# An attention mask and a quantised feed-forward on one core: five instruction orders written anew, and rounding straight to float16

## The reference

```
sim  = (ctx Wq^T)(ctx Wk^T)^T * const             # 512 x 512 per sequence, heads summed
thr  = 153rd largest value of each row of sim
A    = sigmoid(sim) * (sim >= thr);  A = (A + A^T) / 2
x1   = x + (1 - g) * layernorm(x) + g * A           # g = sigmoid(gamma)
y    = layernorm(x1)
bitlinear(v, w): v = rmsnorm(v); v rounded to 255 levels by its row's largest |v|;
                 w rounded to {-1, 0, 1} by mean |w|;  product
out  = x1 + bitlinear(silu(bitlinear(y, w_gate)) * bitlinear(y, w_up), w_down)   # widths 512, 2048, 512
```

## Time and profile before

| | us |
|---|---|
| median of 3 runs (range) | 268.02 (267.92 to 268.54) |
| the profiled execution's own time | 268.02 |
| its span, first to last instruction | 266.2 |
| busy: PE, DVE, ACT, POOL | 216.5, 214.1, 194.6, 169.0 |
| mean granted TensorE clock | 0.91 of full |

### The profile page before, as it was taken

One profiled execution on the slowest core, in us unless ns is written; L12 is line 12 of the kernel. 1 busy time (PEld: TensorE's weight loads), 2 busy tenths in 40 slices (PEclk: granted clock), 3 DMA queues, 4 the chain that ended last, 5 costly groups with the idle time before them and its releaser, 6 DMA issues.

```text
span 266.2 us, 3714 instructions
## 1 busy us (share of the span) xinstructions
PE 216.5 (81%) x962; PEld 107.3 (40%) x974; DVE 214.1 (80%) x376; ACT 194.6 (73%) x333; POOL 169.0 (63%) x322
## 2 busy tenths in 40 slices
PE   7704620225998877999999999999999999999995
PEld 7301300222744432443445444434454444444434
DVE  0585987976869999898899999998898959367881
ACT  2499999899999999996949999736349443654030
POOL 2045787786988646678978878873886812505620
PEclk9965595555799999999999999999999999999999
DMA  4999999999655499420801382330714505743656
GB/s 128 394 374 360 360 230 397 242 317 214 182 113 86 79 178 159 80 59 1 140 1 28 52 139 61 79 68 19 194 37 101 102 0 100 173 133 71 119 101 216
DMA packets 79143, 39.19 MB, mean 147 GB/s; under 512 B 67984, under 2 KB 70544, under 8 KB 78608
## 3 DMA queue, kind: packets, MB, share of 16 engines
q1 hardware_dynamic: 79120, 38.94, 58.9%
HBM read 17.96 MB, written 4.19 MB: 83 GB/s over the span
## 4 chain that ended last, share of the span: by engine, by line
PE 30%; POOL 13%; POOLq 13%; DVE 11%; ACT 10%; issue 9%; DMA 6%; DVEq 4%; SPq 2%; ACTq 0%
PE U L405 9%; PE G L391 9%; PE DN L424 9%; DMA C<-in_ctx 5%; ACT junk_c L514 3%; POOLq L986 3%; ACT WuT L556 2%; POOL S L1047 2%; POOL qx L1016 2%; POOL X L982 2%; ACT S L563 2%; POOLq L948 2%; DVE S L764 2%; POOL sig L939 2%; POOLq L958 2%
## 5 line engine op out<-in xcount | busy, mean ns | idle before, releaser
L391 PE MATMUL G<-WgT,xqT 128*128 128x512 bf16 x256 | 60.5, 379 | 3.6 <-ACT sg L539 3.2
L539 ACT ACTIVATE sg<-G,gsc 128x1024 f32<-128x1024 f32 x32 | 35.5, 1110 | 37.2 <-PE G L391 34.8
L405 PE MATMUL U<-WuT,xqT 128*128 128x512 bf16 x256 | 60.5, 379 | 1.6 <-DVE S L764 1.6
L514 ACT ACTIVATE junk_c<-rows,srch 128x512 int8<-128x512 f32 (+1 forms) x76 | 53.8, 713 | 1.9 <-POOL srch L961 1.2
L764 DVE TENSOR_TENSOR S<-U,sg 128x1024 f32<-128x1024 f32 x31 | 37.9, 1222 | 13.0 <-PE U L405 7.7
L424 PE MATMUL DN<-WdT,S 128*128 128x512 bf16 x197 | 45.5, 379 | 0.9 <-DMA S<-S 0.3
L1047 POOL TENSOR_SCALAR S<-S,qh 128x2048 int16<-128x2048 f32 x15 | 30.0, 2002 | 25.1 <-DVE qh L829 24.9
L391 PEld LDWEIGHTS G<-WgT,xqT 128*128 128x128 bf16 x256 | 24.6, 98 | 35.1 <-issue 3.8
L547 ACT ACTIVATE junk_h<-S 128x2048 int8<-128x2048 f32 x16 | 30.5, 1905 | 10.2 <-DVE S L779 8.6
L405 PEld LDWEIGHTS U<-WuT,xqT 128*128 128x128 bf16 x256 | 24.8, 98 | 32.6 <-DVE S L764 4.3
L769 DVE TENSOR_REDUCE amh<-S 128x1 f32<-128x2048 f32 x15 | 34.1, 2271 | 0.1
(11 more groups left out here) (148 smaller groups left out, 370.4 us busy)
## 6 DMA issues: line engine op xcount, KB each, us to landing
S<-in_L_ffn_w_gate SPq DMA_DIRECT2D x4, 1024.0 KB, 9.2
S<-in_L_ffn_w_up SPq DMA_DIRECT2D x4, 1024.0 KB, 11.9
X<-in_x SPq DMA_DIRECT2D x4, 1024.0 KB, 10.8
S<-in_L_ffn_w_down SPq DMA_DIRECT2D x4, 1024.0 KB, 6.9
out<-X SPq DMA_DIRECT2D x15, 256.0 KB, 2.9
C<-in_ctx SPq DMA_DIRECT2D x2, 256.0 KB, 8.6
C<-in_ctx SPq DMA_DIRECT2D x1, 512.0 KB, 11.5
S<-S SPq DMA_TRANSPOSE x17, 4.3
```

The source lines that it names most:

```text
L391: last = nc.tensor.matmul(G[:, c * 512:(c + 1) * 512], xqT[:, t, k, :], WgT[:, 4 * n:4 * n + 4, k, :], start=(k == 0), stop=(k == KD - 1))
L405: last = nc.tensor.matmul(U[:, c * 512:(c + 1) * 512], xqT[:, t, k, :], WuT[:, 4 * n:4 * n + 4, k, :], start=(k == 0), stop=(k == KD - 1))
L514: A(junk_c[:, j, :].bitcast(U8) if r == ROUNDS else junk_c[:, j, :], ROWS[a % 2][:, j, :], ACT.Sign, bias=nthr[:, j:j + 1], accum_out=cs[: ...
L539: A(sg[:, u % 2, :], G[:, :], ACT.Silu, scale=gsc[:, b % 2, t:t + 1]).then_inc(silu_done, 1)
```

## The change

It has three parts. The number format: values that were rounded to an int16 integer n and then converted to bfloat16 n are now written once as float16 n * 2^-24, a multiple of that type's smallest step, so that the conversion on write does the rounding; the coefficients carry 2^24 in return. The casts `x_cast` and `h_cast` and the second instruction of `last_round` are gone, and those who waited for the int16 version or for the cast wait for the one rounding. Weights and transposed tiles are float16 in place of bfloat16. The orders: the lines of calls of all five engines are new. A wait: `x_stats` of sequence 1 to 3 now waits for the `ln_coef` of the sequence before (`ln_done`), as it can come earlier than before.

```diff
+UNIT = 2.0 ** -24
-        WgT = sb("WgT", [P, F // P, KD, P], BF16)
+        WgT = sb("WgT", [P, F // P, KD, P], F16)
...
-            w_load(0, w_gate, 0); w_load(0, w_gate, 1); w_load(0, w_gate, 2); w_load(0, w_gate, 3)
-            w_load(1, w_up, 0); c_load(0, 1, 2); c_load(1, 2, 4); x_load(0); w_load(1, w_up, 1)
+            w_load(0, w_gate, 1); c_load(0, 1, 2); w_load(0, w_gate, 0); w_load(0, w_gate, 2); w_load(0, w_gate, 3)
+            x_load(0); w_load(1, w_up, 2); x_load(2); w_load(1, w_up, 0); w_load(1, w_up, 1); w_load(1, w_up, 3)
...
                 if js[0] == 0:
                     dve.wait_ge(s_xin[a], 16)
+                    if a:
+                        dve.wait_ge(ln_done, a)
...
-            def x_cast(a, *js):
-                c = slice(js[0], js[-1] + 1)
-                dve.wait_ge(xi_ready, NT * a + js[-1] + 1)
-                V.tensor_copy(qx[:, c, :], qx[:, c, :].bitcast(I16)).then_inc(qx_ready, len(js))
...
-                V.tensor_scalar(hq[:, i % 2, f].bitcast(I16), h[:, i % 2, f], qh[:, i % 4:i % 4 + 1], 1.0,
-                                ALU.mult, ALU.mult)
-                dve.drain()
-                V.tensor_copy(hq[:, i % 2, f], hq[:, i % 2, f].bitcast(I16)).then_inc(hq_last, 1)
+                V.tensor_scalar(hq[:, i % 2, f], h[:, i % 2, f], qh[:, i % 4:i % 4 + 1], UNIT,
+                                ALU.mult, ALU.mult).then_inc(hq_last, 1)
...
-            def h_cast(i):
-                dve.wait_ge(hi_ready, i + 1)
-                V.tensor_copy(hq[:, i % 2, :], hq[:, i % 2, :].bitcast(I16)).then_inc(hq_ready, 1)
...
-                G_.tensor_scalar(gsc[:, a % 2, :], dx, wm[:, 0:1], 1.0, ALU.mult, ALU.mult)
+                G_.tensor_scalar(gsc[:, a % 2, :], dx, wm[:, 0:1], 1.0 / UNIT, ALU.mult, ALU.mult)
...
-                    G_.tensor_scalar(qx[:, j, :].bitcast(I16), ROWS[a % 2][:, j, :], qsx[:, j:j + 1], -1.0,
-                                     ALU.mult, ALU.mult).then_inc(xi_ready, 1)
+                    G_.tensor_scalar(qx[:, j, :], ROWS[a % 2][:, j, :], qsx[:, j:j + 1], -UNIT,
+                                     ALU.mult, ALU.mult).then_inc(qx_ready, 1)
...
-                G_.tensor_scalar(hq[:, i % 2, :].bitcast(I16), h[:, i % 2, :], qh[:, i % 4:i % 4 + 1], 1.0,
-                                 ALU.mult, ALU.mult).then_inc(hi_ready, 1)
+                G_.tensor_scalar(hq[:, i % 2, :], h[:, i % 2, :], qh[:, i % 4:i % 4 + 1], UNIT,
+                                 ALU.mult, ALU.mult).then_inc(hq_ready, 1)
```

More of the change, by code:

```diff
@@ L14 @@
 F32 = mybir.dt.float32
-BF16 = mybir.dt.bfloat16
+F16 = mybir.dt.float16
 I32 = mybir.dt.int32
@@ L457, in _ @@
             pe.wait_ge(s_msb, 1)
[L459 to L463, removed]
@@ L474, in _ @@
-            gate(31); down(11, 0); down(11, 1); up(30); down(12, 0); down(12, 1); up(31); down(13, 0); down(13, 1)
-            down(14, 0); down(14, 1); down_last(0); down_last(1)
+            pre(0); pre_g(0); sims(0, 0); sims(0, 1); sims(0, 2); sims(0, 3); pre(1); pre_g(1); sims(1, 0)
+            w_total(0); sims(1, 1); sims(1, 2); sims(1, 3); w_total(1); miss_total(0); a_transposes(0, 0)
+            a_transposes(0, 1); a_transposes(0, 2); a_transposes(0, 3); pre(2); warm(8, 0); warm(8, 1); gate(0)
@@ new lines, in _ @@
+            pre_g(2); up(0); sims(2, 0); miss_total(1); gate(1); up(1); w_total(2); sims(2, 1); gate(2); up(2)
+            gate(3); up(3); sims(2, 2); gate(4); a_transposes(1, 0); sims(2, 3); gate(5); a_transposes(1, 1); up(4)
+            gate(6); a_transposes(1, 2); a_transposes(1, 3); up(5); gate(7); up(6); down(0, 0); down(0, 1); pre(3)
+            up(7); down(1, 0); down(1, 1); pre_g(3); gate(8); up(8); gate(9); up(9); down(2, 0); gate(10)
+            sims(3, 0); up(10); sims(3, 1); down(2, 1); sims(3, 2); gate(11); down(3, 0); gate(12); sims(3, 3)
@@ new lines, in _ @@
+            add_a(0, 2); add_a(0, 3); ln_coef(1); update(1, 3, 1); x_round(0, 0); lnx(1, 2); x_round(0, 1)
+            lnx(1, 3); x_round(0, 2); x_coef(0); lnx(1, 1); x_round(0, 3); sigmoids(1, 0); lnx(1, 0); sigmoids(1, 1)
+            ln_coef(2); sigmoids(1, 2); add_a(1, 0); lnx(2, 3); sigmoids(1, 3); h_round(0); add_a(1, 1); lnx(2, 1)
+            add_a(1, 2); d_coef(0); first_threshold(2, 0); h_round(1); first_threshold(2, 1); update(2, 0, 0)
+            add_a(1, 3); h_coef(0, 2); h_round(2); x_round(1, 0); update(2, 0, 1); update(2, 1, 0); x_coef(1)
@@ new lines, in _ @@
+            x_round(1, 1); update(2, 1, 1); x_round(1, 2); update(2, 2, 0); lnx(2, 0); x_round(1, 3); d_coef(1)
+            update(2, 2, 1); lnx(2, 2); update(2, 3, 0); ln_coef(3); h_round(3); h_coef(2, 2); update(2, 3, 1)
+            sigmoids(2, 0); h_round(4); sigmoids(2, 1); first_threshold(3, 0); first_threshold(3, 1); sigmoids(2, 2)
+            sigmoids(2, 3); lnx(3, 0); update(3, 0, 0); update(3, 0, 1); add_a(2, 0); add_a(2, 1); add_a(2, 2)
+            add_a(2, 3); lnx(3, 3); h_round(5); h_coef(4, 2); update(3, 1, 0); update(3, 1, 1); sigmoids(3, 0)
```

207 lines of the change are left out of this document (95 added, 112 removed).

## The result

The kernel after takes 272.02 us (271.73 to 273.31, 5 runs) where before takes 268.54 beside it (267.92 to 268.82, 5 runs): ratio 1.0143, interval 1.0127 to 1.0158. It is slower by 3.5 us. I had forecast 263.3 and a chance of 0.12 for slower; the time lies outside my range.

The account below looks back on a forecast made before the run. TensorE's own work was taken to bound 107.4 to 251.0 us, a chain through four queues the first gate. Terms -5.2 + 1.9 + 2.2 - 4.1 + 1.0 - 0.5 = -4.7 gave span 261.5, time 263.3, range 258.5 to 268.0.

Parts of the forecast that it names:

- First gate: Start of TensorE's first gate product: forecast at 68.2 us, worth -5.2 us (ends -1.0 and -6).
- Moved work: Behind the first gate: pre_g(2) and one tile of sims(2) now follow it on TensorE, +1.9 us.
- Clock: TensorE at the first gate: half clock there and some loss behind it, +2.2 us (ends 0 and +5).
- Ramp: TensorE up to the first down: 15 half products by 104.5 us, 2.0 idle taken, -4.1 us (ends -5.1 and 0).
- Full stretch: Where TensorE is full: less room at the first gates of sequences 1 to 3, +1.0 us idle (ends 0 and +5).
- Casts: 25 casts leave VectorE, 16.5 us: worth nothing beside full TensorE, otherwise already counted in ramp and first gate.
- tail: End of the kernel: one cast and a drain leave each half of the last rounding, only -0.5 us.
- Gain eaten: Rival, chance 0.17: xqT again lands after 7.3 us, first gate at 72.4, only -1.0 there, time 267.5.
- slower rival: Chance 0.11: float16 lengthens GpSimd roundings before first gates of sequences 1 to 3, 3.5 us each, time 273.8.
- first rival: Chance 0.22: GpSimd freed from casts, ramp idles only 1 us, clock up at the first gate, time 259.1.

Follow-up runs that it names:

- e7_first_gate: Orders of before with float16 format, plus first gate brought forward (x load later, second warm group gone, x_coef(0) earlier): 268.57 us, ratio 1.0002 to before.
- e8_muls: Kernel after with two moves on VectorE, mul(11) in front of threshold(2) and final(3) behind mul(12): 273.06 us, ratio 1.0163 to before.
- e13_less_dve: Kernel after with VectorE's four masks of sequence 2 and final(2) to final(4) cut to 8 of 512 columns: 269.19 us, ratio 1.0028 to before.
- e16_less_pool: Kernel after with GpSimd's sigmoids and additions of A of sequence 2 cut to 8 of 512 columns: 268.98 us, ratio 1.0027 to before.
- e14_less_dve_old: Orders of before with float16 format, masks of sequence 2 and final(2) to final(4) cut to 8 of 512 columns: 267.12 us, ratio 0.9947 to before.
- e1_format: Kernel after with the five order lines of before, less the names of the casts: 267.67 us, ratio 0.9973 to before.
- e9_pool: Kernel after with three moves on GpSimd: update(2, 3, 1) and h_round(3) before ln_coef(3), h_round(4) straight behind h_coef(2, 2): 272.93 us, ratio 1.0185 to before.
- e10_warm: Kernel after with six more warm products on TensorE behind the second group, before the first gate: 272.20 us, ratio 1.0153 to before.

## Why the prediction was wrong

**First gate, -5.2.** It was -1.4. SyncE was the late party, as I said, but it started its four weight transposes 3.3 us late, 1.2 of it from ahead of the last mask and 2.0 from the wait of 3.04 for GpSimd, and took 0.9 more for them. Worse, I counted the earlier gate in full: in the orders of before e7_first_gate brought the gate forward by 2.4 us and the end not at all.

**Moved work, +1.9.** The two products are there, within the first window; at 0.86 us between starts each they are 1.7.

**Clock, +2.2.** In the profiled execution the clock is 0.94 over the first window and gate(0) took 3.60. In e8_muls, with the same wait, it took 1.90 and the window shows 1.00; gate(8) came 0.8 sooner. TensorE was busy 45.74 us in that window of after and 43.38 in that of e8_muls, so the low clock cost 2.4 of busy time when it came, near my 2.2, but more than half of that only filled idle time. The term is at most about 1, and of the ten traces with the orders of after, or nearly, five show the first gate at 1.90.

**Ramp, -4.1.** 15 half products were done at 110.73, 38.7 us behind the first gate, where I forecast 36.3; up to gate(8) TensorE idled 2.9 where I took 2.0, and where before had idled 6.4. This part was near. With the first gate late, all of it together gave 1.7 in place of 5.2.

**Full stretch, +1.0 (ends 0 and +5).** This is the step that failed: it cost 6.8. I wrote that VectorE "was not late either" since it was busy 122.70 of 143.60 us, and looked for lost room only at three gates. At these three, gate(8), gate(16) and gate(24), TensorE waits for no xqT at all. From an average over 143 us no order can be judged. The new order pulls gates and ups forward by putting off sequence 2, and so binds VectorE and GpSimd to each other where a `mul` has little slack: e13_less_dve and e16_less_pool give back 2.8 and 3.0 of the time, e14_less_dve_old nothing in that stretch. So I had put at nothing that the ranks and masks put off must then be done between `mul`s that TensorE waits for. For the part of the 6.8 behind gate(16), 2.6, the cause stays open.

**Casts, tail.** The casts beside full TensorE are worth nothing in the old orders, as I said; in the new ones they are worth 9.7 us. The tail gained 0.5 up to `down_last(0)`, as forecast (the wait of 0.64 in the earlier trace rows is gone), and 0.6 was lost behind it, in an execution whose last store landed later than in most of the others.

**Rivals.** "Gain eaten" had the first gate right (72.4 against 72.02), for another reason: the transpose landed in 2.6 and was issued late. Float16 on GpSimd cost nothing. The slower rival put its loss at the first gates of sequences 1 to 3, by a longer rounding; TensorE waits for xqT at none of them, and the loss lies between. No rival named the work put off.

## What to carry to other kernels

Before you credit an earlier start, ask whether the second step starts earlier too; if it waits for another engine, the start is worth nothing. Judge a new order by the work that it puts off: list for each stretch of some 20 us what stands on the helping engines, and compare that with the room between two steps of the engine that should be full. Where single moves don't help, take work away from one engine at a time: that tells the short engine from the one that merely shows as busy.

The fastest kernel here that leaves nothing out is the new format in the old orders, e1_format: 0.27% under before and 1.7% under after.

## What the runs showed of the hardware

A `scalar_tensor_tensor` on VectorE with both inputs in SBUF takes 0.69 us for 512 columns alone and 1.76, 2.24 and 1.96 beside a rounding of 1.97 us on GpSimd, whose own time doesn't change (1.97 in each of the three). In e9_pool the rounding ended at 139.90 and the rank at 140.45. The Trainium skill (SBUF — State Buffer, "Who interferes with whom") says that a VectorE instruction with two SBUF inputs contends with a GpSimd instruction that reads SBUF and that whoever comes second is blocked; the trace agrees, and here it is VectorE that waits. In after the rank of 2.24 likewise ended 0.54 behind its rounding. The prediction named this direction only in passing, against its first rival, and gave it no term. The other direction shows too: in after a GpSimd sigmoid of 512 columns took 1.27 at 139.02, beside the rank of 0.69 at 139.13, where the shortest of the sixteen took 0.76. Over the whole span the effect on VectorE is not small: the 16 masks and 12 ranks, the same instructions, take 3.0 us longer in after.

```profile
L678 DVE SCALAR_TENSOR_TENSOR sig<-rows,srch,sig 128x512 f32<-128x512 f32 x16 | 14.4, 928 | 2.5 <-issue 1.9 <-POOL sig L927 0.7
L629 DVE SCALAR_TENSOR_TENSOR mask<-junk_c,rows 128x512 f32<-128x512 uint8 x12 | 11.9, 994 | 2.5 <-ACT junk_c L515 2.2
```

and in e1_format:

```profile
L679 DVE SCALAR_TENSOR_TENSOR sig<-rows,srch,sig 128x512 f32<-128x512 f32 x16 | 12.4, 807 | 3.0 <-issue 1.5 <-POOL sig L929 1.3
L630 DVE SCALAR_TENSOR_TENSOR mask<-junk_c,rows 128x512 f32<-128x512 uint8 x12 | 10.9, 909 | 3.2 <-ACT junk_c L515 2.7
```

This is 3.0 of the 3.2 us by which VectorE is busier in after (204.2) than in e1_format (201.0). How much of the loss it makes, no run tells apart from the order itself. Moving the rounding away from one rank put it beside the next, and the time didn't fall.

The level of TensorE's clock at the first gate differs between executions with nearly the same wait in front: 3.60 us for eight products behind 2.86 us of waiting (after), 2.70 behind 2.25 (e10_warm), 1.90 behind 3.28 (e8_muls). What decides it these runs don't show.
